# Keys of two cross attentions: three copies of 32 rows in one transfer with a repeated source

## The reference, cut to what matters

```python
# layer 0: keys and values are the context itself, a capped softmax, a mask per key
u = jnp.einsum('hbqd,hbkd->hbqk', q, k) * scale / np.sqrt(d_k)
logits = jnp.tanh(u) * jnp.exp(log_C)
attn = jax.nn.softmax(jnp.where(mask, -jnp.inf, logits), axis=-1)
out = jnp.einsum('hbqk,hbkd->hbqd', attn, v)     # then  @ W_out.T
# layer 1: keys and values are projections of the context
k = _split_heads(key @ Wk.T + bk)
v = _split_heads(value @ Wv.T + bv)
scores = jnp.einsum('bhqd,bhkd->bhqk', q, k) / jnp.sqrt(jnp.float32(DK))
p = jax.nn.softmax(jnp.where(mask, scores, jnp.float32(-1000000000.0)), axis=-1)
out = jnp.einsum('bhqk,bhkd->bhqd', p, v)        # then  @ Wo.T + bo
```

## Time and profile before

| | us |
|---|---|
| median of 3 runs | 703.43 (700.96 to 706.05) |
| the profiled execution | 700.59 |
| its span, first to last instruction | 698.8 |
| first cross attention, first key score to last one | 15.8 to 259.6 |
| second cross attention, first key score to last one | 345.0 to 544.5 |

### The profile page before, as it was taken

The page is one execution under the profiler, slowest core; times in us unless marked ns, Lnnn a source line. Parts: engine busy times, 40 slices in busy tenths (PEclk is TensorE's granted clock), DMA queues, the critical chain, the costliest instruction groups (busy, mean ns, idle before and its releaser), DMA issues. The chain is left out here.

```text
span 698.8 us, 14299 instructions
## 1 busy us (share of the span) xinstructions
PE 618.0 (88%) x5014; PEld 374.2 (54%) x5014; DVE 407.2 (58%) x899; ACT 453.5 (65%) x543; POOL 69.1 (10%) x151
## 2 busy tenths in 40 slices
PE   6888887887887888796799999999999998898998
PEld 5554444444344444464345555555554575674886
DVE  6467354222313225876798989898884326645634
ACT  2988999999999993682057767676777215503111
POOL 3001110000010000101211121211110000000000
PEclk8899999999999999998889999999999999999999
DMA  5886786376444113200027633322220570000000
GB/s 132 234 254 206 237 237 211 102 232 173 132 131 127 58 46 118 52 1 3 1 74 248 182 93 81 84 77 86 75 86 10 168 239 1 2 0 1 0 1 15
DMA packets 52904, 73.57 MB, mean 105 GB/s; under 512 B 11044, under 2 KB 29796, under 8 KB 52860
## 3 DMA queue, kind: packets, MB, share of 16 engines
q1 hardware_dynamic: 52091, 72.25, 35.0%
q10 hardware_dynamic: 768, 0.73, 0.4%
HBM read 58.90 MB, written 12.85 MB: 103 GB/s over the span
## 5 line engine op out<-in xcount | busy, mean ns | idle before, releaser
L1704 DVE TENSOR_REDUCE sb_m_blk<-ps 128x1 f32<-128x512 f32 x256 | 159.5, 684 | 18.5 <-PE ps L1550 17.2
L1486 ACT ACTIVATE sb_probs<-ps 128x1024 f32<-128x1024 f32 x128 | 125.8, 1025 | 49.9 <-PE ps L1580 49.3
L656 ACT ACTIVATE sb_probs<-ps 128x1024 f32<-128x1024 f32 x128 | 124.0, 1023 | 10.4 <-PE ps L721 8.9
L661 ACT ACTIVATE sb_probs<-sb_probs,sb_neg_cap,sb_cap 128x4096 f32<-128x4096 f32 (+2 forms) x34 | 121.9, 3591 | 0.1
L740 PE MATMUL ps<-sb_probs,sb_v_st 128*32 128x256 f32 x1024 | 74.5, 388 | 37.2 <-ACT sb_probs L661 37.2
L721 PE MATMUL ps<-sb_q_st,sb_k_st 112*128 112x256 bf16 x512 | 79.3, 280 | 5.2 <-DMA sb_k_st<-k_parts_l 4.4
L1580 PE MATMUL ps<-sb_q_st,sb_k_st 115*128 115x256 bf16 x512 | 76.3, 272 | 1.4 <-ACT sb_probs L1486 1.4
L1550 PE MATMUL ps<-sb_k_st,sb_q_m 96*128 96x512 bf16 x224 | 76.5, 383 | 0.0
L721 PEld LDWEIGHTS ps<-sb_q_st,sb_k_st 112*128 112x128 bf16 x512 | 42.9, 99 | 58.3 <-issue 28.9
L1596 PE MATMUL ps<-sb_probs,sb_v_st 128*32 128x256 f32 x1024 | 67.4, 384 | 0.2 <-ACT sb_probs L1486 0.2
L740 PEld LDWEIGHTS ps<-sb_probs,sb_v_st 128*32 128x32 f32 x1024 | 23.7, 108 | 64.8 <-ACT sb_probs L661 45.5
(11 more groups left out here) (284 smaller groups left out, 846.6 us busy)
## 6 DMA issues: line engine op xcount, KB each, us to landing
sb_k_st<-k_parts_l SPq DMA_DIRECT2D x223, 64.0 KB, 2.0
sb_k_st<-k_parts_l SPq DMA_DIRECT2D x93, 128.0 KB, 3.2
k_parts_l<-sb_v_proj SPq DMA_DIRECT2D x24, 256.0 KB
k_parts_l<-sb_early SPq DMA_DIRECT2D x48, 128.0 KB
sb_v_proj<-ctxT_blocks SPq DMA_DIRECT2D x8, 512.0 KB, 7.0
sb_v_rows<-ctx_by_pair SPq DMA_DIRECT2D x7, 512.0 KB, 4.2
sb_early<-ctxT SPq DMA_DIRECT2D x6, 512.0 KB, 3.8
sb_k_st<-k_parts_l SPq DMA_DIRECT2D x64, 32.0 KB, 1.8
```

The costliest lines, as they stand in the source:

```text
L656: a.activation(probs[:, slot, 4 * g:4 * g + 4, :], scores_bank(g), ACT.Tanh).then_inc(s["tanh"], 1)
L661: a.activation(part, part, ACT.Exp, bias=k.neg_cap[:, 0:1], scale=k.cap[:, 0:1]).then_inc(s["exp"], 1)
L1486: sc.activation(probs[:, g], scores_bank(g), ACT.Exp).then_inc(s["exp"], 1)
L1704: v.tensor_reduce(k.m_blk[:, b, q, blk:blk + 1], k.ps[:, m_bank(m_turn_of(idx)), :], AX.X, ALU.max).then_inc(s["m_read"], 1)
```

## The change

The three equal transfers become one, whose source is the 32 rows with a repeat of 3 in front (stride 0) and whose destination is rows 0 to 95. In the first cross attention the two blocks of a unit then take a transfer each, because the source's two counts and the block count no longer fit one, so a unit has three transfers where it had four. In the second a quarter has two where it had four. The waits count accordingly (`K0_LOADS` = 3, `K_LOADS1` = 2). The bytes moved are the same, and each piece of memory moved at once is still one row of 1024 bf16, 2048 bytes.

```diff
     rows = unit.rearrange("b s d n -> (s d) b n")
     dst = k.k_st[:, slot, :].rearrange("p (b n) -> p b n", n=KSPLIT)
-    for r in range(PARTS):
-        sp.dma_start(dst[2 * DH * r:2 * DH * (r + 1)], rows[0:2 * DH]).then_inc(loaded, 16)
+    for b in range(2):
+        thrice = rows[0:2 * DH, b].unsqueeze(0).to_broadcast([PARTS, 2 * DH, KSPLIT])
+        sp.dma_start(dst[0:MAXROW, b], thrice).then_inc(loaded, 16)
     sp.dma_start(dst[MAXROW:STACK0], rows[2 * DH:3 * DH]).then_inc(loaded, 16)
+
+
+K0_LOADS = 3
@@
-                    pe.wait_ge(k_in[j], 16 * K_LOADS * (it if j == 0 else it + 1))
+                    pe.wait_ge(k_in[j], 16 * K0_LOADS * (it if j == 0 else it + 1))
@@
-K_LOADS1 = PARTS + 1
+K_LOADS1 = 2
@@ def load_k1_quarter(k, sp, h, b, quarter, loaded):
-    for r in range(PARTS):
-        sp.dma_start(dst[2 * DH * r:2 * DH * (r + 1), :], src[0:2 * DH, :]).then_inc(loaded, 16)
+    thrice = src[0:2 * DH, :].unsqueeze(0).to_broadcast([PARTS, 2 * DH, QUARTER])
+    sp.dma_start(dst[0:MAXROW, :], thrice).then_inc(loaded, 16)
     sp.dma_start(dst[LOROW:STACK, :], src[2 * DH:3 * DH, :]).then_inc(loaded, 16)
```

## The result

| | us |
|---|---|
| median after, 6 runs | 786.4 (782.1 to 788.3) |
| median before, 6 runs beside it | 703.2 (698.2 to 706.1) |
| ratio | 1.117 (95% interval 1.113 to 1.121) |
| span of the profiled execution after | 784.9 |
| first cross attention, first key score to last | 16.8 to 327.1: 310.3, before 243.8 |

The kernel is 12% slower. By stages the profiled executions differ by +66.5, +1.9 and +16.6 us, and by +1 us ahead of the first score, 86.1 us together; the medians differ by 83.2. The +1.9 can't be told from chance: in the other kernels run here this stretch took 84.8 to 88.0 us, and 88.0 is that of a kernel whose loads there are those of before (`first_merged`).

What follows compares the result with a forecast made beforehand. Keys did not limit the kernel before; merged, three DMA engines would carry all wide transfers and be the limit. 38 (first cross attention) + 18 (second) + 5 (SP) = 61 us on 700.6, so 763 us by median, range 722 to 840.

Steps and rivals of the forecast that it cites:

- The price of a piece: Time of one 2048-byte piece on one of three DMA engines: 88 ns taken, bounds 80 and 113 ns.
- Some of it is absorbed once: 15 us: First cross attention: key slots loaded three units ahead, 23 us less landing time, would hide 15 us of excess work.
- surplus of 53 us: First cross attention: three engines must carry 265 us of work in 212 us, 53 too much.
- 38 + 5: Forecast loss of the first cross attention, +38 us, plus +5 us for SP's waits for stores.
- +5 for SP: SP's waits for stores, with key loads behind them: about 2 us at each of five places, 0 to +10.
- 8 x 2.8: Preloads of heads 0 and 1 need 23 us of the three engines from 270 us, hidden by the self attention.
- The loss lies ahead of 180 us: First cross attention: from 180 us on demand just equals the 51 us there, so the loss falls earlier.
- +18 forecast: Second cross attention: 185 us of work in 164 less 3 us of slack, lost in the first six heads.
- What would show it: Marks listed beforehand: small packets per transfer, landing times, TensorE's key waits, unit period, DMA share, unchanged other stages.
- All 16 engines: Rival: only the destination's 96 rows decide, so transfers use every engine, about 701 us; chance 0.09.
- Quick: Rival: three engines at 80 ns a piece, only the first cross attention late, about 730 us; chance 0.17.
- Slow: Rival: three engines reading the same row stay at 113 ns a piece or above, 830 to 862 us; chance 0.14.

Runs made afterwards that it cites:

- first_merged: Kernel before, only first cross attention merged, repeat as second source count, first unit's high and middle rows also three at once: 701.8 us beside 701.8, ratio 0.999.
- spread: Changed kernel's wide transfers, same size and number, with the repeat as second source count and query stack rows reordered: 706.9 us, ratio 1.009 to the kernel before.
- two_copies: Changed kernel with two of the three copies in one wide transfer and the third plain: 803.5 us, ratio 1.144 to the kernel before.
- late_wide: Kernel before with wide transfers only for units 16 to 31 of the first cross attention, narrow ones by block: 716.6 us, ratio 1.019.
- early_wide: Kernel before with wide transfers only for units 1 to 15 of the first cross attention, narrow ones by block: 745.9 us, ratio 1.061.
- half_wide: Changed kernel with only block 0 of each unit and quarters 0 and 2 of each head wide, the rest plain: 734.2 us, ratio 1.048 to the kernel before.

## Why the prediction was right, and where it was short

- **Direction and mechanism: right and shown.** Three engines (3 small packets a wide transfer, `spread` with 16 and the loss gone, `two_copies` with 2 and more loss). The measured 786 us lies in the range 722 to 840, 23 us above the 763 forecast.
- **The price of a piece: 88 ns taken, somewhat low.** Where three engines work alone, 76 GB/s is 81 ns. Under load it is more. In 19 to 298 us of the changed kernel the queue's share is 44.4% of 16 engines:

```profile
q1 hardware_dynamic: 23204, 39.36, 44.4%
```

  0.444 x 279 x 16 = 1982 us of engine time. If three engines are busy throughout (837 us), the other thirteen have 88 us each, near the 85 + 31 x 0.2 of the prediction, and wide keys take 279 - 88 = 191 us of each of the three: 6.2 us a unit, 96 ns a piece. That is an estimate, and its premise was not measured by engine. The packet records of the trace do not speak against it: from 22 to 298 us fewer than three packets are under way for 9 us only, and the 2048-byte packets of the stage took 99 ns on average (median 84).
- **"Some of it is absorbed once: 15 us": the term that was wrong.** The lead of the key slots was taken as a reserve of the whole stage. It protects one buffer, and other transfers on the same three engines have nearly none: `late_wide` lost 14 us with the keys in time, through the context block.
- **The sum with both terms put right.** The surplus of 53 us grows by 16 for the price (31 x 64 pieces x 8 ns) and falls by 3 for the other loads (88 us for 91): 66 us, nothing absorbed, and 66.5 were measured. This is bookkeeping and no test, because the price was found by taking the three engines as busy for the whole stretched stage. The tests are `late_wide` and `early_wide`. The prediction's 38 + 5 falls short by 13 us for the price and the other loads and by 15 for the lead, and its +5 for SP is not needed: SP's waits for stores grew only from the 17 us of the earlier trace rows to 20.0 (11.5 + 8.5).
- **Small points of the working.** 8 x 2.8 is 22 and not 23 us. The 1.4 us in the landing time of a wide transfer stands in no row; the shortest landing of a plain one is 1.8 us.
- **"The loss lies ahead of 180 us": nearly.** Unit 24 was issued at 176.6 us before and at 235.6 after, 59 of the 66 us; 8 more came with TensorE's next wait for a context block (5.9 us at 243 us).
- **Second cross attention: +18 forecast, +16.6 measured,** in the heads with late weights as said (15.4 us a head against 12.2, forecast 15 against 12), nothing behind them. Here the 3 us of lead and 88 ns gave the right sum. How far that is luck is open: no run tests either term in this stage, and `half_wide` shows that a sum by engine work is not the whole account there either.
- **What would show it.** Small packets 3: yes. Waits for keys: 29.4 us in the first, where over 35 was forecast, beside 32 us for the context and value blocks; 10.8 in the second (over 10). Period of a unit, from one exp to the next: 11.1 us on average up to 177 us (over 8.5 forecast), behind it mostly 7.5 to 7.6 (near 7.7), but 22.0 and 14.8 in the two units with the longest waits for a context block. Share lower though DMA is the limit: 0.39 for 0.68 in 150 to 180 us. Landing times of the wide transfers are not given in the view, so that mark stays unread. Self attention and the stages behind: +1.9 us, within what other runs show, and +0.1.
- **The rivals.** All 16 engines fell by the packets. "Quick" fell by the time, 786 for 730 us, though its 80 ns is what the rate gives where three engines work alone. "Slow" with 113 ns a piece (830 us and more) fell too; the estimate of 96 ns lies between it and the 88 taken.

## What to carry to other kernels

Before merging transfers, read the first count of both access patterns: here a repeat of three in front put everything on three DMA engines, and the same repeat as the second count kept all sixteen. Then sum the work of the busiest engine by stretches, not over the stage, and compare it with each stretch's length. A lead counts only for the buffer that has it: look for the transfer with the smallest lead that shares the engine.

## What the runs showed of the hardware that I had not expected

- SP's issue takes longer for a wide transfer and depends on its shape: 0.31 us at least for 32 plain rows, 0.51 for two copies of 32 on two engines, 0.56 for 32 rows three times on 16 engines, 0.71 for three copies of 32 on three. One merged issue is worth about two plain ones, not three.
- Overloaded DMA engines seem to hold the issuing engine, which is a reading and was not tested: L417's issue, 0.33 us at least, had a median of 1.6 and a maximum of 5.1 us in the changed kernel, so SP's other work behind it, for whatever engines, was late too.
- One DMA engine moves 2048-byte rows from memory at 25.3 GB/s where three work alone (76 GB/s). Beside the other loads of the first cross attention it is some 96 ns a row, 21 GB/s, by the estimate above.
